# Maxima and reciprocals spread to all lanes over memory, with the pipeline one slot deeper

## The reference

```
q = layernorm(x) @ Wq + bq;  k, v = ctx @ Wkv + bkv
p = softmax(q k^T / sqrt(128));  o = p v
x = x + tanh(g_xattn) * (concat(o) @ Wo + bo)
x = x + tanh(g_ffn) * (layernorm(x) @ base_W^T + 2 * top2-routed LoRA)
```

## Time and profile before

| | us |
|---|---|
| median of the runs | 2336.35 (2335.97 to 2344.81) |
| profiled run, device time | 2337.85 |
| its span | 2335.9 |
| TensorE busy | 2289.8 |
| VectorE, ScalarE, GpSimd busy | 1822.1, 1685.2, 1631.9 |

### The profile page before, as it was taken

The page is one execution under the profiler, slowest core; times in us unless marked ns, Lnnn a source line. Parts: engine busy times, 40 slices in busy tenths (PEclk is TensorE's granted clock), DMA queues, the critical chain, the costliest instruction groups (busy, mean ns, idle before and its releaser), DMA issues.

```text
span 2335.9 us, 37750 instructions
## 1 busy us (share of the span) xinstructions
PE 2289.8 (98%) x12569; PEld 1956.9 (84%) x12569; DVE 1822.1 (78%) x3162; ACT 1685.2 (72%) x3208; POOL 1631.9 (70%) x1372
## 2 busy tenths in 40 slices
PE   7999999999999999999999999999999999999988
PEld 6888888888888888888888888888888888888864
DVE  5887888879778787877878778787878768778775
ACT  4776777767777776777767777776777767777763
POOL 5897987967667786866757867774865757656672
PEclk9999999999999999999999999999999999999999
DMA  7444334354133233335133243223423122122211
GB/s 256 147 147 142 117 129 144 133 201 144 59 124 114 93 122 100 98 108 185 59 104 105 77 133 115 102 92 115 143 82 109 66 79 82 46 100 73 82 37 54
DMA packets 122591, 258.11 MB, mean 111 GB/s; under 512 B 13344, under 2 KB 46624, under 8 KB 122144
## 3 DMA queue, kind: packets, MB, share of 16 engines
q1 hardware_dynamic: 122400, 255.71, 32.4%
HBM read 188.81 MB, written 66.86 MB: 109 GB/s over the span
## 4 chain that ended last, share of the span: by engine, by line
PE 87%; DVE 5%; POOL 4%; ACT 2%; issue 2%; DMA 0%; ACTq 0%; SPq 0%; POOLq 0%; DVEq 0%
PE psW L381 13%; PE psW L382 12%; PE psW L383 12%; PE psW L577 7%; PE psS L383 7%; PE psS L381 7%; PE psS L382 7%; PE psW L579 7%; PE psW L578 7%; PE psW L436 2%; PE psW L444 2%; POOL xs L766 2%; POOL pl L770 1%; DVE mrun L1194 1%; DVE psum_ L1221 1%
## 5 line engine op out<-in xcount | busy, mean ns | idle before, releaser
L766 POOL TENSOR_TENSOR xs<-xs,mb 128x512 f32<-128x512 f32 (+1 forms) x832 | 1069.2, 1314 | 518.1 <-ACT mb L837 518.1
L1194 DVE TENSOR_TENSOR mrun<-psS,mrun 128x512 f32<-128x512 f32 (+1 forms) x704 | 483.9, 687 | 380.3 <-ACT xs L837 377.7
L837 ACT ACTIVATE xs<-psS 128x512 f32<-128x512 f32 (+1 forms) x832 | 496.7, 597 | 212.2 <-PE psS L383 202.6
L930 ACT ACTIVATE ph<-xs 128x512 fp32r<-128x512 f32 (+1 forms) x832 | 520.6, 626 | 0.9 <-PE psW L579 0.9
L991 DVE TENSOR_TENSOR pl<-psP,ph 128x512 fp32r<-128x512 f32 (+1 forms) x672 | 459.5, 684 | 54.8 <-ACT ph L930 49.0
L1221 DVE TENSOR_TENSOR psum_<-psP,psum_ 128x512 f32<-128x512 f32 (+1 forms) x672 | 457.3, 681 | 0.0
L927 ACT ACTIVATE psP<-xs 128x512 f32<-128x512 f32 (+1 forms) x672 | 402.4, 599 | 3.0 <-POOL xs L766 1.5
L381 PE MATMUL psS<-ql,kh 128*128 128x512 f32 (+1 forms) x832 | 344.1, 414 | 1.1 <-DVE ql L1014 1.1
L577 PE MATMUL psW<-ph,vh 128*128 128x512 f32 (+1 forms) x832 | 336.6, 405 | 5.8 <-POOL pl L770 4.0
L383 PE MATMUL psS<-qh,kl 128*128 128x512 f32 (+1 forms) x832 | 328.1, 394 | 0.0
L382 PE MATMUL psS<-qh,kh 128*128 128x512 f32 (+1 forms) x832 | 328.1, 394 | 0.0
(11 more groups left out here) (185 smaller groups left out, 4562.5 us busy)
## 6 DMA issues: line engine op xcount, KB each, us to landing
wqh<-scr_wq SPq DMA_DIRECT2D x96, 256.0 KB, 2.6
wql<-scr_wq SPq DMA_DIRECT2D x96, 256.0 KB, 2.9
woh<-scr_wo SPq DMA_DIRECT2D x48, 512.0 KB, 3.3
wol<-scr_wo SPq DMA_DIRECT2D x48, 512.0 KB, 4.4
scr_wq<-wqh SPq DMA_DIRECT2D x32, 256.0 KB, 2.0
scr_wq<-wql SPq DMA_DIRECT2D x32, 256.0 KB, 2.5
scr_wo<-woh SPq DMA_DIRECT2D x16, 512.0 KB, 2.6
scr_wo<-wol SPq DMA_DIRECT2D x16, 512.0 KB, 4.0
```

The costliest lines, as they stand in the source:

```text
L766: eng.tensor_tensor(tile, tile, mb[0:rows_of(t), U % 2, :], ALU.subtract).then_inc(s_sub)
L837: return eng.activation(hi, src, ACT.Copy)
L930: eng.activation(ph[0:rows, T % RP, :], xs[0:rows, T % RX, :], ACT.Exp).then_inc(s_h)
L1194: eng.tensor_tensor(run, psS[0:rows, s % 2, :], a, ALU.max).then_inc(s_m)
```

## The change

From unit 16 on, the maxima (up to unit 61) and the reciprocals (up to unit 60) are not spread by TensorE and copied by ScalarE. SP writes the [128, 4] result to a scratch in memory, waits for the write, and reads it back as one row of 512 to all 128 lanes, into mb and rbc. So that the 512 values come in order, the turn before it takes every fourth column (`every_fourth`). A second table, AT_MEM, has no r, and its b is skipped; on_slot moves the multiplication from slot 8 to 9, and the output jobs move back with it. The reduction of the maxima moves to slot 0, that of the sums to the front of slot 6. SUB, EXP, VAL and RX rise by one, and mrun has one buffer instead of two. In the first batch r of the first row of AT shares a slot with v0. The loads of output weights and some stores and fetches of cut parts are moved to slot 3. The diff without the semaphores' names and the scratch's declaration:

```diff
--- before.py
+++ after.py
...
-    SUB, EXP, VAL = 16, 17, 19
-    RX, RP = 19, 4
+    SUB, EXP, VAL = 17, 18, 20
+    RX, RP = 20, 4
     SLOTS = NT * (UN + 2)
...
+    MEM_LO, MEM_MAX, MEM_SUM = 16, UN - 2, UN - 3
+    def max_by_mem(U):
+        return MEM_LO <= U < MEM_MAX
+    def sum_by_mem(U):
+        return MEM_LO <= U < MEM_SUM
+    def by_pe(U, by_mem):
+        return sum(not by_mem(u) for u in range(U + 1))
+    def on_slot(V):
+        return 9 if sum_by_mem(V) else 8
     jobs = {s: [] for s in range(SLOTS)}
     AT = [
-        "m q0 b k3 q1 s v0 r v1 v2 o0 v3 o1",
+        "m q0 b k3 q1 s - r,v0 v1 v2 o0 v3 o1",
         "m,v4 v5 b,q0 v6 k0 s q1 r k1 v7 o0,v8 v9 o1,v10",
...
     ]
+    AT_MEM = [
+        "m q0 b k3 q1 s - v0 v1 v2 v3 o0 o1",
+        "m,v4 v5 b,q0 v6 k0 s,v7 q1 k1 v8 v9 v10 o0 o1",
+        "m,v11 k2 b,v12 q0 k3 s - - q1 - - o0,x0 o1,x1",
+        "m q0 b k0 q1 s k1 - - k2 - o0 o1",
+    ]
     for U in range(UN + 2):
         names_of = {0: "k1 - k2 v0 q0 k3 q1 v1 - v2 - v3 -", UN: "- - - - - s - r - - o0 - o1",
-                    UN + 1: "- - - - - s - r - - o0 o1"}.get(U, AT[U % 4])
+                    UN + 1: "- - - - - s - r - - o0 o1"}.get(U, (AT_MEM if U >= 2 and sum_by_mem(U - 2) else AT)[U % 4])
         for t, names in enumerate(names_of.split()):
...
                 if not 0 <= n < top or (kind == "x" and U % NU < 14):
+                    continue
+                if kind == "b" and max_by_mem(n) or kind == "r" and sum_by_mem(n):
                     continue
...
     order = [p for p, s in cut_at]
+    def kept_at(z):
+        return z + 4 if z > NT * NU and z % NT == 12 else z + 1
...
         if no >= len(first) + 2:
-            s = max(s, at - 10, cut_at[last][1] + 1)
+            s = max(s, at - 10, kept_at(cut_at[last][1]))
             assert s <= at, (p, at, s)
...
         cst = sb("cst", [128, 512], F32R)
-        mrun = sb("mrun", [128, 2, 512], F32)
+        mrun = sb("mrun", [128, 512], F32)
         pp = sb("pp", [128, 2, 512], F32)
...
-            def turn(key, src, done, by, v):
+            def turn(key, src, done, by, v, every_fourth=False):
                 o = take(key)
                 for k in range(4):
-                    m = eng.transpose(o[:, k * 128:(k + 1) * 128], src[:, k * 128:(k + 1) * 128], ident[:, :])
+                    cols = src.rearrange("l (p k) -> l k p", k=4)[:, k, :] if every_fourth else src[:, k * 128:(k + 1) * 128]
+                    m = eng.transpose(o[:, k * 128:(k + 1) * 128], cols, ident[:, :])
                 m.then_inc(done)
...
                     pe.wait_ge(s_m, 12 * (n + 1))
-                    turn(("m", n, 0), mrun[:, n % 2, :], s_mt, s_nm, n + 1)
+                    turn(("m", n, 0), mrun[:, :], s_mt, s_nm, n + 1, max_by_mem(n))
                 elif kind == "s":
...
                         pe.wait_ge(s_ap, 2 * (n - NU + 1))
-                    turn(("s", n, 0), psum_[:, n % 2, :], s_su, s_r, n + 1)
+                    turn(("s", n, 0), psum_[:, n % 2, :], s_su, s_r, n + 1, sum_by_mem(n))
                 elif kind == "b":
                     pe.wait_ge(s_nm, n + 1)
-                    spread(("b", n, 0), nm[:, n % 2, :], s_bt, s_mb, n + 1)
+                    spread(("b", n, 0), nm[:, n % 2, :], s_bt, s_mb, by_pe(n, max_by_mem))
                 elif kind == "r":
                     pe.wait_ge(s_r, n + 1)
-                    spread(("r", n, 0), rinv[:, n % 2, :], s_rt, s_rb, n + 1)
+                    spread(("r", n, 0), rinv[:, n % 2, :], s_rt, s_rb, by_pe(n, sum_by_mem))
                 elif kind == "x":
...
                     eng.matmul(o, vl[0:rows, t, hs], hi, start=False, stop=t == NT - 1).then_inc(s_pv)
-                if s % NT == 10 and s // NT >= 2:
+                if s // NT >= 2 and s % NT == on_slot(s // NT - 2) + 2:
                     emptied(("pv", s // NT - 2, 0), s_ol, s // NT - 1)
...
                 eng.dma_start(f32(cl[:, :, lo:lo + w]), scr_c[b - 1, 1, :, :, lo:lo + w]).then_inc(s_lc[c], 16)
+            def max_to_lanes(n):
+                i = n - MEM_LO
+                sp.wait_ge(s_nm, n + 1)
+                if i >= 2:
+                    sp.wait_ge(s_md, 16 * (i - 1))
+                eng.dma_start(scr_m[n % 2], nm[:, n % 2, :]).then_inc(s_mw, 16)
+                sp.wait_ge(s_mw, 16 * (i + 1))
+                if n >= 2:
+                    sp.wait_ge(s_sub, NT * (n - 1))
+                eng.dma_start(mb[:, n % 2, :], scr_m[n % 2].rearrange("p k -> (p k)").partition_broadcast(128)).then_inc(s_md, 16)
+            def sum_to_lanes(n):
+                i = n - MEM_LO
+                sp.wait_ge(s_r, n + 1)
+                if i >= 2:
+                    sp.wait_ge(s_rd, 16 * (i - 1))
+                eng.dma_start(scr_r[n % 2], rinv[:, n % 2, :]).then_inc(s_rw, 16)
+                sp.wait_ge(s_rw, 16 * (i + 1))
+                if n:
+                    sp.wait_ge(s_on, n)
+                eng.dma_start(rbc[:, :], scr_r[n % 2].rearrange("p k -> (p k)").partition_broadcast(128)).then_inc(s_rd, 16)
...
                 b, u = divmod(U, NU)
-                for kind, n, part in cuts.get(s - 1, []):
+                if t == 1 and max_by_mem(U - 1):
+                    max_to_lanes(U - 1)
+                if t == 6 and sum_by_mem(U - 2):
+                    sum_to_lanes(U - 2)
+                for kind, n, part in [p for z in (s - 4, s - 1) if kept_at(z) == s for p in cuts.get(z, [])]:
                     if kind == "c":
...
                         load("v", n + 1, 4, s_v, NT * n + NT)
-                    elif kind == "o" and part == 1 and NU <= n + 1 < UN:
+                    elif kind == "o" and part == 1 and NU <= n + 1 < UN and not sum_by_mem(n):
                         load("o", n + 1, NU, s_o, 2 * n + 2)
...
                         load_ctx(n // 8 + 1, part)
+                if t == 3 and sum_by_mem(U - 3):
+                    load("o", U - 2, NU, s_o, 2 * (U - 3) + 2)
                 if u == 14 and t == 1 and b + 1 < B:
...
                 U, t = divmod(T, NT)
-                pool.wait_ge(s_mb, U + 1)
+                if max_by_mem(U):
+                    pool.wait_ge(s_md, 16 * (U - MEM_LO + 1))
+                else:
+                    pool.wait_ge(s_mb, by_pe(U, max_by_mem))
                 pool.wait_ge(s_e, T + 1)
...
                     elif kind == "b":
-                        act.wait_ge(s_bt, n + 1)
+                        act.wait_ge(s_bt, by_pe(n, max_by_mem))
                         if n >= 2:
...
                     elif kind == "r":
-                        act.wait_ge(s_rt, n + 1)
+                        act.wait_ge(s_rt, by_pe(n, sum_by_mem))
                         if n:
...
                 V = s // NT - 2
-                if s % NT == 8 and 0 <= V < UN:
+                if 0 <= V < UN and s % NT == on_slot(V):
                     act.wait_ge(s_on, V + 1)
...
                 if n >= 2:
-                    dve.wait_ge(s_bt, n - 1)
+                    dve.wait_ge(s_bt, by_pe(n - 2, max_by_mem))
+                    if max_by_mem(n - 2):
+                        dve.wait_ge(s_mw, 16 * (n - 2 - MEM_LO + 1))
                 eng.tensor_reduce(nm[:, n % 2, :], bank_of(("m", n, 0)).rearrange("p (j k) -> p j k", j=4),
...
                     if n >= 2:
-                        dve.wait_ge(s_rt, n - 1)
+                        dve.wait_ge(s_rt, by_pe(n - 2, sum_by_mem))
+                        if sum_by_mem(n - 2):
+                            dve.wait_ge(s_rw, 16 * (n - 2 - MEM_LO + 1))
                     settle(eng.tensor_reduce(ssum[:, n % 2, :], bank_of(("s", n, 0)).rearrange("p (j k) -> p j k", j=4),
...
             dve.wait_ge(s_tg, 1)
+            def goes_first(kind, n, part):
+                return kind == "s" and sum_by_mem(n)
             for s in range(SLOTS):
...
                 b, u = divmod(U, NU)
+                for j in jobs.get(s - 1, []):
+                    if goes_first(*j):
+                        after_job(*j)
                 if s < TN:
                     rows = rows_of(t)
-                    run = mrun[0:rows, U % 2, :]
+                    run = mrun[0:rows, :]
                     if t:
...
                         if t == 1:
-                            if U >= 2:
-                                dve.wait_ge(s_mt, U - 1)
+                            if U:
+                                dve.wait_ge(s_mt, U)
                             a = xs[:, (s - 1) % RX, :]
...
                         eng.tensor_tensor(run, psS[0:rows, s % 2, :], a, ALU.max).then_inc(s_m)
-                if t == 8 and 0 <= U - 2 < UN:
-                    V = U - 2
+                V = U - 2
+                if 0 <= V < UN and t == on_slot(V):
                     dve.wait_ge(s_pv, NT * (V + 1))
-                    dve.wait_ge(s_rb, V + 1)
+                    if sum_by_mem(V):
+                        dve.wait_ge(s_rd, 16 * (V - MEM_LO + 1))
+                    else:
```

(15 more changed lines are left out.)

## The result

The kernel after takes 2412.87 us in the median (2409.10 to 2417.14), the kernel before, on the same chip, 2337.57: a ratio of 1.032 (1.029 to 1.034). Slower, as forecast, but by 75 us instead of 12, and outside the range of 2324 to 2371. The profiled run took 2417.14 us with a span of 2415.2, so 79.3 us more span than before. All times and ratios here are of executions in the chip's faster state; one of the five of norm_strided, 4211.79 us at a granted clock of 0.863, was not.

A forecast was written before the change was run, and what follows sets the result against it. TensorE, busy for 98% of the span, was taken to bound the kernel. The terms -40.0 + 29.0 + 16 + 8 - 5 + 3 + 1 - 1 + 1 gave +12 us, so 2348.4 us, range 2324 to 2371.

The forecast's parts named there:

- The gain, -40.0: On TensorE, 46 spreadings of maxima and 45 of reciprocals taken out, 0.44 us each: 40.0 us less.
- The slot deeper is what costs: In slot 5, the turn of the sums waits for GpSimd's merge by 1.1, 1.1, 0.4, 0.03 us in kinds 0, 3, 1, 2: +29.0.
- The later waits, +16, +8 and -5: Rest of each unit after the turn, on TensorE: +16 us in kind 2, +8 in kind 3, -5 in kind 1.
- Kind 3's term: Units with U mod 4 = 3: value product 0.2 us late, output product waiting 0.5 us for ol; 0.7 x 11 = 8 us.
- Small things: First batch's reciprocals +3 us, unit 63's merge wait +1, shorter stall in unit 57 -1, tail +1.
- Both are taken at nothing: Maxima and reciprocals sent over memory arrive before GpSimd and VectorE want them, so their waits cost 0.
- The cover of 7.1 us: Time from the reciprocals being ready to VectorE wanting them in the tightest kind: 7.1 us.
- The 5.5 us: Assumed time for write and read over memory, from a range of 4.6 to 8.2 us plus some 0.5 for issues.
- C: Rival: queue late, 8.2 + 0.5 us in place of 5.5, reciprocals miss VectorE; 24 us more, 2372 us; chance 0.10.
- I take 0: TensorE's turns loading every fourth column cost nothing, as a slower load has room behind the matmul spacing.
- the upper end of 20 us: Strided loads of 91 turns taking twice as long with half exposed: 20 us.
- the cases faster by over 0.5%: Outcomes below 2324.7 us, given a chance of 0.12, against 0.36 within 0.5% and 0.52 slower.

The follow-up runs named there:

- norm_strided: Kernel after, heavy jobs also a slot back, reciprocals with U mod 4 = 0 by TensorE, last batch's norms on every second column: 2327.42 us, ratio 0.995.
- whole_shift_maxima: whole_shift with the maxima of units 16 to 61 spread over memory, the reciprocals by TensorE: 2392.7 us.
- shallow_sums: Kernel before at its own depth, with reciprocals over memory in 33 units, not where U mod 4 is 0, maxima by TensorE: 2330.2 us, ratio 0.996.
- whole_shift: Kernel after with all spreading by TensorE; turn of the sums, reciprocals, multiplication and output jobs one slot back too, heavy jobs not: 2411.66 us, ratio 1.032.
- true_shift: Kernel after with all spreading by TensorE, turn of the sums and what follows a slot back, heavy jobs too: 2351.25 us, ratio 1.005.
- fetch_after_sums: Kernel after with the context fetches of slots 3 to 6 moved to slot 7, behind the reciprocals' store and broadcast: 2388.45 us, ratio 1.021.
- after_but_one_kind: Kernel after with the reciprocals of units where U mod 4 is 0 spread by TensorE again: 2361.7 us, ratio 1.010.

## Why the prediction was right in sign and wrong in size

**The gain, -40.0.** In the slots it is right within some 10%: those with another job lose 0.44 to 0.48 us with a spreading (3.26 to 2.82 in slot 2 of kind 1), slots without one 0.36 (1.75 to 1.39 in kinds 0 and 3), as they are held by other engines anyway. That a unit gets shorter by as much was assumed for both kinds of spreading and is shown for the maxima (19 us in whole_shift_maxima). For the reciprocals shallow_sums gave 8 of 14.5 us, since the output job behind them waited instead.

**"The slot deeper is what costs", +29.0.** Right as a mechanism, in place and in size: for the matmuls themselves 28.3 us in 34 waits, where some 33 at 0.9 us had been announced. What was missing is what it means. I took the wait for one term that could be moved; whole_shift moved it and it came back as waits for pl. true_shift shows that it belongs to a chain that must stay beside the heavy slots.

**The later waits, +16, +8 and -5.** By unit, spreadings included, the forecast was +0.22, -0.94, +0.45 and +0.92 for kinds 0 to 3; measured +0.49, -0.75, +0.73 and +1.64. Kind 3's term is the one most mis-sized: slot 9 of unit 35 lasts 4.13 us (its k2 with the products takes 3.5) and slot 11, with o0, 3.41 instead of 2.77, together 1.3 us where I had 0.7. For undisturbed units it makes 16 us more than forecast in all: 3.0 + 2.1 + 3.4 + 7.9. In kind 2 the reciprocals over memory never paid: +0.73 with them, -0.42 without. "Small things" and the ends: +3.3 against +4.

**"Both are taken at nothing".** This failed, and it is the largest part. The cover of 7.1 us was right: in fetch_after_sums the rows of units 38 and 42, landed 7.5 and 7.8 us after the write's issue, are waited for by 0.3 and 0.6 us, and earlier ones of that kind are not. The landing was right too, where the queue is quiet: from the issue of the write to the landing of the read 5.2 to 7.7 us in 35 units. In the ten others, 20, 22, 26, 30, 36, 38, 40, 42, 46 and 62, it is 10.0 to 13.3. The read is not what varies (3.2 to 4.7 us, median 3.7); the write is, from 1.4 to 9.6 (median 2.3). Writes and reads together:

```profile
DMA to landing us min/median/max: 1.4/3.4/9.6
```

The 5.5 us came from medians of large transfers, and I noted of the moved fetches only that GpSimd had room for them, not that SyncE stands for a landing in front of one and that six loads then go out ahead of the reciprocals. The chance of 0.10 for C was too small, and its price too, 24 us by unit kinds: it cost some 38 us in six units, 5 in units 20, 36 and 40 and 2 in unit 62. Part of the price is half clock after each stall of the seven units, in no term of the sum. This is the step that failed: a wait put at nothing that cost some 45 us. Without it the kernel after would have come out near 2368 us, slower than before and inside the range, so the sign was not luck.

**"I take 0" for the strided turn.** 4 to 6 us. The Trainium skill, "SBUF — State Buffer", section "Specifications (TRN2)", which asks for two hits on each 16-byte line, was right in direction: loads of 203 and 210 ns against 141. It hides for the most part behind matmuls, and the upper end of 20 us was far off.

**Unit 62, in no term:** 7 to 8 us with a norm that GpSimd holds up. In the kernel after VectorE's next maximum comes late by it, and TensorE stands for 5.7 us. No run took the hold away and left all else as it was; in whole_shift, where the norm takes 0.61 us, the unit is 1.2 us longer than before, no more than the others of its kind there (1.1).

The account: 12 forecast, +16 in undisturbed units, +45 by the queue (half clock included), +7.6 for the norm, -1 at the ends; 79.6 against 79.3. As the parts are lengths read from one trace, their sum had to close; that after_but_one_kind came out at 2361.7 us, with 2360 expected from them, is the test. A slip of no weight in the chances: the cases faster by over 0.5% add up to 0.11, not 0.12, the slower ones to 0.53, not 0.52.

## What to carry to other kernels

When one engine's chain is moved by a slot against a hand-made table, move the heavy entries of the table with it; here a wait that was moved alone turned up again at the next consumer of the same chain. Before a small transfer is put on the path, read the queue that it joins, instruction by instruction, in the worst unit: what the issuing engine stands for ahead of it, and how many bytes go out just before it. The median landing tells nothing about that, and leaving out the quarter of the units that collide gave back 51 us, more than the 40 that all the transfers were to save.

## What the hardware showed beyond the forecast

- A 2 KB write lands after 1.4 us on a quiet queue and after 7.0 us behind 2 MB of loads (9.6 us at most in the run); the read of the row to all 128 lanes after 3.2 to 4.7 us in every unit.
- After a stall of 4.4 us with 0.48 us of work, TensorE ran 5.5 us at a granted clock of 0.5, products 0.43 us apart; before and behind it, 0.23.
- VectorE's TENSOR_SCALAR with source and result in SBUF stood for 6.9 to 7.2 us beside GpSimd's tensor_tensor instructions without a gap, at 512, at 8 and at 512 strided columns, until the last of them had ended (7.8 us in the kernel after). The next one of the same form took 0.53 us. In true_shift and whole_shift such an instruction got through between two of GpSimd's, after 0.61 to 1.61 us. The Trainium skill, "SBUF — State Buffer", section "Who interferes with whom", tells of a pair of ports that VectorE and GpSimd share and that such an instruction has to have alone; that fits, and no run here shows the ports themselves, nor why VectorE was passed over up to six times in one row and not in another.
